# Four normalised columns split over two steps of ScalarE, and the square root placed ahead of a cast, in a fused convolution and FFN kernel

## What is computed

```python
x = x + conv_ref(_ln_c(x))        # depthwise 3x3 convolution per channel, plus its input
t = x.reshape(B, H * W, C)
t = t + ffn_ref(_ln_t(t))         # relu(_qlinear(t, W1, b1)), then _qlinear(., W2, b2); 96 -> 384 -> 96
```

## Time and profile before

| what | value |
|---|---|
| time, median of 3 runs | 3998.27 us (3997.37 to 4000.93) |
| the profiled execution's own time | 3986.89 us |
| its span, first to last instruction | 3985.2 us |
| mean granted TensorE clock | 0.967 of full |
| DVE, PE, ACT, POOL busy | 91%, 79%, 73%, 43% of the span |

### The profile page before, as it was taken

How to read it: one execution, slowest core, us unless ns; L and a number is a source line. 1 busy time by engine, 2 the same in 40 slices (tenths; PEclk the granted TensorE clock), 3 DMA queues, 4 the chain that set the end, 5 groups by cost and what they waited for, 6 DMA issues and landing times.

```text
span 3985.2 us, 87474 instructions
## 1 busy us (share of the span) xinstructions
PE 3157.9 (79%) x24902; PEld 2493.7 (63%) x24902; DVE 3609.6 (91%) x12635; ACT 2925.6 (73%) x6204; POOL 1719.3 (43%) x915
## 2 busy tenths in 40 slices
PE   3488888878887888878888787887888888889977
PEld 3376666666666666666666666666666666667744
DVE  6558999999999999999999899998999999999998
ACT  4457777777777777777777777777777777776765
POOL 0003444444444444444444444444444444445555
PEclk9999999999999999999999999999999999999955
DMA  4566666656666666666666666666666666665533
GB/s 135 179 175 182 189 186 189 189 173 189 189 186 187 179 185 189 186 187 189 185 189 184 181 189 186 189 186 174 189 187 189 187 189 190 191 190 171 164 107 92
DMA packets 277355, 714.63 MB, mean 179 GB/s; under 512 B 34809, under 2 KB 34914, under 8 KB 276834
## 3 DMA queue, kind: packets, MB, share of 16 engines
q1 hardware_dynamic: 276834, 708.57, 60.6%
HBM read 539.84 MB, written 168.59 MB: 178 GB/s over the span
## 4 chain that ended last, share of the span: by engine, by line
PE 54%; ACT 31%; issue 7%; DMA 4%; DVE 1%; ACTq 1%; SPq 1%; POOL 0%; POOLq 0%; DVEq 0%
PE conv_ps L390 33%; ACT images L473 14%; PE hid_ps L355 13%; ACT hid L452 9%; PE y_ps L368 7%; ACT y L460 4%; ACT xt L444 4%; DMA band_ring<-bands 3%; DMA xn<-in_x 1%; ACTq L171 1%; DVE stats L593 0%; PE conv_ps L333 0%; PE xt_ps L342 0%; DVE images L574 0%; SPq L270 0%
## 5 line engine op out<-in xcount | busy, mean ns | idle before, releaser
L390 PE MATMUL conv_ps<-images,band_ring 112*112 112x222 f32 (+1 forms) x9216 | 2058.5, 362 | 512.6 <-ACT xt L444 382.1
L390 PEld LDWEIGHTS conv_ps<-images,band_ring 112*112 112x112 f32 x9216 | 1563.0, 178 | 805.6 <-issue 550.8
L452 ACT ACTIVATE hid<-hid_ps 128x896 f16<-128x896 f32 x1344 | 1225.4, 912 | 504.4 <-PE hid_ps L355 504.4
L232 POOL TENSOR_TENSOR xf<-xf,images 112x768 f32<-112x768 f32 x448 | 979.8, 2187 | 1263.8 <-DVE hid L582 893.2
L238 POOL TENSOR_TENSOR xf<-xf,y 112x768 f32<-112x768 f32 x448 | 736.2, 1643 | 997.9 <-DVE y L613 997.9
L637 DVE SCALAR_TENSOR_TENSOR xq<-xf,stats,xt_ps 112x96 fp8e5<-112x96 f32 x3584 | 844.3, 310 | 0.0
L368 PE MATMUL y_ps<-w2t,hid 128*128 128x96 f16 x10752 | 634.7, 211 | 173.9 <-ACT y L460 172.3
L368 PEld LDWEIGHTS y_ps<-w2t,hid 128*128 128x128 f16 x10752 | 554.9, 100 | 329.3 <-ACT y L460 213.3
L473 ACT ACTIVATE images<-xn,neg_mean,rstd 112x96 f32<-112x96 f32 x1792 | 723.0, 544 | 14.3 <-DVE neg_mean L629 14.2
L355 PE MATMUL hid_ps<-xt,w1t 96*128 96x448 fp8e5 x2688 | 694.6, 368 | 27.9 <-ACT xt L444 19.4
L460 ACT ACTIVATE y<-y_ps 112x384 f16<-112x384 f32 x896 | 443.2, 495 | 363.6 <-PE y_ps L368 362.0
(11 more groups left out here) (46 smaller groups left out, 604.3 us busy)
## 6 DMA issues: line engine op xcount, KB each, us to landing
band_ring<-bands SPq DMA_DIRECT2D x768, 294.0 KB, 5.2
xn<-in_x SPq DMA_DIRECT2D x448, 336.0 KB, 3.5
xf<-in_x SPq DMA_DIRECT2D x448, 336.0 KB, 4.8
out<-xf SPq DMA_DIRECT2D x448, 336.0 KB, 3.9
bands<-images SPq DMA_DIRECT2D x4, 3528.0 KB, 13.6
xf<-in_L_ffn_W SPq DMA_DIRECT2D x2, 144.0 KB, 2.8
xf<-in_L_conv_kernel SPq DMA_DIRECT2D x3, 3.4 KB
xf<-in_L_ffn_b SPq DMA_DIRECT2D x1, 42.0 KB, 3.2
```

The lines of the kernel that those rows point to most:

```text
L232: pool.tensor_tensor(x2, x2, images[:, b, i, :, cols].rearrange("p c w -> p w c"), ALU.add).then_inc(with_conv, 1)
L390: mm = pe.matmul(dst[:, :, lo:hi], band_ring[:, n % BAND_RING, PAIR * dx + i, :], images[:, m % 2, :, ch, lo + dx - 1:hi + dx - 1], start= ...
L452: nc.scalar.activation(hid[:, c % 2, TOK * j:TOK * (j + 1)].rearrange("p (u n) -> p u n", u=2), hid_ps[:, k, :, 0:HALF * H], ACT.Identity) ...
```

## The change

The four columns that ACT normalises are done in two parts. Columns 0 and 1 stay where all four were, at the end of the chunk's step. Columns 2 and 3 move into the next step of ACT, behind `copy_xt` and ahead of the first save; only they now report the chunk as normalised (`normed[0]`). And `deviation`, the square root, stands ahead of the FFN's first cast instead of behind it. No instruction is added or removed; DVE, PE, POOL and SP keep their programs.

```diff
+ACT_NOW = 2
...
-                def normalise(r, c):
+                def normalise(r, c, lo, hi):
                     e = c - NORM_AT
                     b, i, cols = chunk_at(e)
-                    wait(act, neg_done, LOOP * r + e + 1)
-                    wait(act, with_conv, LOOP * r + e - LOOP + 1)
...
+                    if lo == 0:
+                        wait(act, neg_done, LOOP * r + e + 1)
+                        wait(act, with_conv, LOOP * r + e - LOOP + 1)
...
-                    for w in range(ACT_COLS):
+                    for w in range(lo, hi):
...
-                    op.then_inc(normed[0], 1)
+                    if hi == ACT_COLS:
+                        op.then_inc(normed[0], 1)
...
                     if now:
                         copy_xt(r, c)
+                    if norm_in(t - 1):
+                        normalise(r, c - 1, ACT_NOW, ACT_COLS)
                     save_conv(r, c - 1, t - 1, 3, C)
+                    if ffn_in(t + 1) or norm:
+                        deviation(r, c, t)
                     if now:
                         cast_hid(r, c, 0)
-                    if ffn_in(t + 1) or norm:
-                        deviation(r, c, t)
...
                     if norm:
-                        normalise(r, c)
+                        normalise(r, c, 0, ACT_NOW)
```

More of the change, by code:

```diff
@@ L462, in cast_y @@
                                          ACT.Identity).then_inc(y_cast, 1)
-                def normalise(r, c):
+                def normalise(r, c, lo, hi):
                     e = c - NORM_AT
                     b, i, cols = chunk_at(e)
-                    wait(act, neg_done, LOOP * r + e + 1)
-                    wait(act, with_conv, LOOP * r + e - LOOP + 1)
-                    if e == STAGED_FROM:
-                        for s in bands_out:
-                            act.wait_ge(s, 16)
-                    for w in range(ACT_COLS):
+                    if lo == 0:
+                        wait(act, neg_done, LOOP * r + e + 1)
+                        wait(act, with_conv, LOOP * r + e - LOOP + 1)
+                        if e == STAGED_FROM:
+                            for s in bands_out:
+                                act.wait_ge(s, 16)
+                    for w in range(lo, hi):
                         op = nc.scalar.activation(images[:, b, i, :, cols.start + w], xn[:, e % NORM_RING, w, :],
```

## The result

The changed kernel takes 4111.87 us (median of 4 runs, 4094.61 to 4140.73) against 3997.82 of the kernel before on the same chip: 1.0293 of its time, 95% interval 1.0263 to 1.0323. It is slower by some 114 us, where 103 us less was predicted. The profiled execution took 4110.1 us, its span is 4108.4 and the mean granted clock 0.925, where it was 0.967 before. The lines of the code are 1 to 5 higher than before: L391 is the convolution (L390), L445 the copy of `xt`, L453 the cast of `hid`, L475 the columns, L593 `quantise`, L598 the statistics.

What follows compares the result with a forecast made beforehand. The prediction took PE and ACT as the bound at 8.32 us a step, with DVE close at 7.72. Its terms, -175 + 23 + 49 = -103 on 3998.3, gave 3895 us, with 3838 to 3960 for 8 in 10.

Steps and rivals of the forecast that it cites:

- the band path: Steady part: late column report delays SP's bands; 16.27 us per two steps, taken as 16.17, 7.88 a step; gain 175 us.
- The gap from xn to the band: On SP in the steady part: the first band goes out 1.46 us after xn.
- The start of a unit: Every 28 steps, 13 times: late POOL sum and PE waiting for moved columns cost 1.8 us each, 23 us lost.
- Rival (3): Steady part: bands late in nearly every step, 8.13 us each; 3996, or 4054 with landing 6.0; chance 0.12, 0.09 of it slower.
- Rival (1): Steady part: bands arrive in time and DVE sets the pace, 0.60 us a step won; 3836 us; chance 0.15.
- Rival (2): Band-building steps ahead of the FFN lose nothing, the load having time to spare; 3846 us; chance 0.08.
- Rival (4): Steady part: columns don't shorten the chain, PE waiting at the late cast; 0.1 to 0.3 us more a step, 3935 to 4000; chance 0.1.
- the root's zero: Steady part: moving ACT's square root ahead of the first cast changes the time by 0, bounds 0 and 0.1 us a step.
- the early steps' term: Band-building steps ahead of the FFN: xn's load goes out later, 2.56 us more in each of 19 steps, 49 us lost.
- the columns' term: Steady part: two columns leave the PE and ACT chain, 0.72 us off 8.32, giving 7.60 a step.
- DVE's floor: Steady part: DVE's own work, without its wait for the root, allows no step shorter than 7.72 us.

Runs made afterwards that it cites:

- half dose of fillers: Changed kernel plus four useless PE matmuls (eight instructions) ahead of the band's wait in two steps of seven: 4002.12 us, 1.0021 of the kernel before.
- with the bands ahead: Changed kernel with SP issuing the first band of a step ahead of xn and its wait for the columns: 3852.43 us, 0.9642 of the kernel before.

## Why the prediction was wrong, point by point

**The sum's sign failed in one term**, the band path in the steady part, and in it at the price of PE's work behind the wait: "I take 5.6 for these, 16.17 and 7.88 a step". The path itself was right in each piece: two of seven steps wait, xn's issue comes 1.49 after the copy (1.50), PE starts 5.63 after the band's issue (5.70, taken as 5.6), and where the clock was kept two steps are 16.28. What stood in the sum at a fixed price was PE's work behind the wait, "the first channel runs without a break, six matmuls of 0.188" and "it is what it was: 4.19": those durations come from a trace in which PE waited 0.38. Behind a wait of 2.11 they ran at half clock in 15 of 28 cases, and 7.61 became 9.74. Over all 28 that is 1.18 us a case more; 28 of 93 in 390 steps are 117 cases, so 138 us of the 217 that were missed, and more than the forecast gain of 103. The half dose of fillers gives 110 to 134 by experiment.

**The gap from xn to the band** was 1.65 on average instead of 1.46, mostly since `out` took 1.3 to 1.5 us to issue in 3 of the 28 cases (0.9 to 1.5 in 7 of all 94 steps), and never over 0.6 in the kernel before in the same stretch: 0.19 x 117 = 22 us. In the long step above, `out` alone took 1.48.

**The start of a unit** was taken at 1.8 us, 23 in all. The step in which PE waits for the moved columns took 10.5 us against 7.6 of the others, 2.9 x 13 = 38 us, since here too PE's work behind a wait was priced at full clock. Two such steps with the clock kept took 9.2 and 9.3 us, near the 1.8; those with half clock took up to 12.5. That is 15 us more.

These three are 138 + 22 + 15 = 175 of 217; what remains, some 40 us, is not assigned. The mean of `quantise` went from 1129 ns to 1236, 48 us in all, since POOL's sum fell over it more often, where the sum had this at the unit starts alone. How much of it lies on the path is not shown: in the run with the columns alone it stayed at 1130, and that kernel lost as much. DVE's 210.8 us of waiting for ACT's late casts overlap the first of the three and can't be added.

**Small readings.** 8.32 - 7.88 is 0.44, 172 us and not 175. From the `y` cast at 2012.15 to the copy of `xt` at 2012.65 are 0.50; the 0.39 is right for the cast at 2017.85, and so is the step of 8.32. At the unit's start of the earlier trace rows, POOL's sum lies over `quantise` for 2180.19 + 2.18 - 2180.64 = 1.73 us and costs it 1.51, so not quite the whole overlap was lost.

By the Trainium skill, DMA: Bandwidth & Descriptors, section Anatomy of one DMA, the 2.0 us and 436 GB/s that the prediction quotes are for transfers that GpSimd issues. Those here are SP's: the 2.7 us that it gives for a band is near the shortest landing of the earlier trace rows, 2.8, and about half of the median, 5.2. No term of the sum went by it.

**The rivals.** Rival (3), the band path in nearly every step, was nearest in time (3996 to 4054) and on the right side, and was wrong as a mechanism: it is two steps of seven, each dearer. It was priced by the landing, and the landing was never the surprise. Rival (1) was a real kernel, one edit of SP away: 3836 forecast, 3852 measured. That it came so near has luck in it. The 390 steps won 158 us where the rival has 0.60 x 390 - 23 = 211, and ahead of the FFN only 18 were lost instead of 49, since the earlier bands help there too. Rival (2) fell: the early steps did lose what was forecast, 49 us by experiment and 45 in the trace. Rival (4) fell: with the bands ahead PE and ACT are off the chain (11% and 4%), so the columns did shorten it.

**What was right**: the root's zero (1.0004), the early steps' term, DVE's wait for the root gone, statistics every 6.7 us, waits for bands in two of seven steps, and the other steps at the 7.60 of the columns' term: 45 of the 93 took 7.6, which is under the 7.72 taken for DVE's floor. "Within 0.2 or slower" had been given 0.13 in all, for a change whose price lies in a queue that was already waited for in the trace before: a row with a wait of 0.38 us was read as a cost, and it was a margin that had run out.

By the Trainium skill, TensorE: Matmul & The Clock Gate, section HAM oscillation — how this bites in real kernels, a kernel that waits for a transfer in each tile has its clock drop to half in the wait and begins the next tile slow. The trace agrees in kind, and with shorter waits than the 3 to 5 us of that section's example: 15 of the 28 waits were followed by half clock, those of 2.11 us on average, and the others of 1.53 were not.

## What to carry to other kernels

A semaphore that is reported later is paid by everything that stands behind its wait in the queue: write down that queue, and before shortening the chain move ahead what doesn't need the report. Where a sum puts a wait of some us on TensorE, price its work behind the wait at both clock levels; and the cheapest test is to put useless work in the wait's place. When one floor goes, look for the transfer that now starts relatively later (here xf) and for what its consumer will lie over.

## What the runs showed of the hardware

Useless matmuls made a kernel faster: 8 instructions of 0.19 us in each of 119 steps took 4112 to 4002 us, while the same instructions cost 24 us where PE had nothing to wait for. Behind a wait for a band the half clock either did not come (13 cases, 1.00 over six us) or cost 1.7 us (11 cases, 0.72) or 2.8 to 3.2 (4 cases, 0.50 to 0.52), and nothing lay between. All eight waits for a band of 2.1 to 2.8 us were followed by it, and 7 of the 20 shorter ones. The length of the wait alone does not decide: of twelve waits of 2.06 to 2.10 us for the moved columns, 8 were followed by it and 4 were not.

SP's issue of a 336 KB transfer, 0.33 us as a rule, took 0.9 to 1.5 us in 7 of 94 steps of the changed kernel; in 95 steps of the kernel before, the longest was 0.60. What makes it long is open: in the run with only a later report it was 1 of 89.
